# Ten effective feed-forward weights made during attention, and another order of copies and sums around the first layer norm's slices

## The reference

```python
Q = (layernorm(x) @ Wq.T).reshape(b, s, 8, 4, 128)
K = (ctx @ Wk.T).reshape(b, s, 8, 128)
V = (ctx @ Wv.T).reshape(b, s, 8, 128)
probs = softmax(where(causal, einsum('bqhed,bkhd->bheqk', Q, K) * scale, min))
x = x + tanh(g_xattn) * (einsum('bheqk,bkhd->bqhed', probs, V).reshape(b, s, 4096) @ Wd.T)

def linear(x, w, su, sv):              # su: (rows, 4), sv: (4, columns)
    return einsum('bsh,oh->bso', x, w * (su @ sv))
h = layernorm(x)
d = silu(linear(h, gate...)) * linear(h, up...)       # 1792 hidden units
x = x + tanh(g_ffn) * linear(d, down...)
```

## Time and profile before

| | us |
|---|---|
| median of 3 runs | 1369.67 (1368.61 to 1370.26) |
| the profiled execution | 1369.36 |
| its span, first to last instruction | 1367.6 |
| PE busy | 1359.0 (99%) |
| DVE busy | 960.1 (70%) |
| POOL busy | 955.9 (70%) |
| ACT busy | 561.9 (41%) |
| granted TensorE clock, mean | 1.000 |

### The profile page before, as it was taken

How to read it: one execution, slowest core, us unless ns; L and a number is a source line. 1 busy time by engine, 2 the same in 40 slices (tenths; PEclk the granted TensorE clock), 3 DMA queues, 4 the chain that set the end, 5 groups by cost and what they waited for, 6 DMA issues and landing times.

```text
span 1367.6 us, 21475 instructions
## 1 busy us (share of the span) xinstructions
PE 1359.0 (99%) x7794; PEld 1114.2 (81%) x7794; DVE 960.1 (70%) x1467; ACT 561.9 (41%) x952; POOL 955.9 (70%) x883
## 2 busy tenths in 40 slices
PE   9999999999999999999999999999999999999998
PEld 9988788888888878777787877788888888888887
DVE  6587776675555676676667877774789888766776
ACT  6455555545344432232323433332344434334333
POOL 5699999999887946445554666573787787666664
PEclk9999999999999999999999999999999999999999
DMA  8486777777978866453454556621322331311121
GB/s 294 138 266 203 252 251 252 262 244 242 341 252 284 293 228 222 153 167 124 153 171 140 185 158 197 200 71 39 78 62 62 93 85 47 123 54 47 48 69 70
DMA packets 158201, 226.47 MB, mean 166 GB/s; under 512 B 43280, under 2 KB 89872, under 8 KB 156048
## 3 DMA queue, kind: packets, MB, share of 16 engines
q1 hardware_dynamic: 157952, 224.83, 51.3%
q10 hardware_dynamic: 144, 0.26, 0.1%
HBM read 155.32 MB, written 69.73 MB: 165 GB/s over the span
## 4 chain that ended last, share of the span: by engine, by line
PE 83%; POOL 11%; DVE 2%; issue 2%; ACT 1%; DMA 1%; SPq 0%; DVEq 0%; ACTq 0%; POOLq 0%
PE bank L620 65%; POOL wa_lo L1702 5%; PE bank L898 4%; PE bank L900 4%; PE bank L899 4%; PE bank L776 4%; PE bank L752 3%; POOL ws L1690 1%; POOL ws L1693 1%; POOL ws L1691 1%; POOL ws L1695 1%; DVE xc L1291 1%; PE bank L667 0%; POOL xb L1671 0%; DMA er_raw<-in_sf_r 0%
## 5 line engine op out<-in xcount | busy, mean ns | idle before, releaser
L620 PE MATMUL bank<-xc,wa_hi 128*128 128x512 f32 x896 | 277.8, 391 | 0.8 <-ACT s L1023 0.8
L620 PE MATMUL bank<-wd_hi,o_hi 128*128 128x512 f32 x512 | 202.9, 396 | 0.5 <-issue 0.5
L620 PE MATMUL bank<-wd_lo,o_hi 128*128 128x512 f32 x512 | 199.6, 390 | 0.0
L620 PE MATMUL bank<-wd_hi,o_lo 128*128 128x512 f32 x512 | 199.2, 389 | 0.0
L620 PEld LDWEIGHTS bank<-xc,wa_hi 128*128 128x128 f32 x896 | 167.3, 188 | 38.0 <-ACT s L1023 2.6
L620 PE MATMUL bank<-xc,wa_lo 128*128 128x512 f32 x448 | 174.6, 390 | 0.0
L1074 ACT ACTIVATE o_hi<-bank 128x512 fp32r<-128x512 f32 x128 | 69.5, 595 | 228.3 <-PE bank L776 151.1
L1494 DVE SCALAR_TENSOR_TENSOR X<-bank,tg,X 128x512 f32<-128x512 f32 x221 | 154.4, 741 | 0.0
L620 PE MATMUL bank<-x_hi,wf_hi 128*128 128x512 f32 x392 | 152.7, 389 | 0.1
L620 PE MATMUL bank<-x_hi,wf_lo 128*128 128x512 f32 x392 | 152.5, 389 | 0.0
L620 PE MATMUL bank<-x_lo,wf_hi 128*128 128x512 f32 x364 | 141.7, 389 | 0.0
(11 more groups left out here) (182 smaller groups left out, 3160.8 us busy)
## 6 DMA issues: line engine op xcount, KB each, us to landing
q_scratch<-q_st SPq DMA_DIRECT2D x32, 1024.0 KB, 5.0
q_sb<-q_scratch SPq DMA_DIRECT2D x64, 512.0 KB, 4.7
w_raw<-in_wq SPq DMA_DIRECT2D x32, 512.0 KB, 4.3
wd_raw<-in_wd SPq DMA_DIRECT2D x16, 1024.0 KB, 4.9
f_raw<-ffn_eff_scratch SPq DMA_DIRECT2D x28, 512.0 KB, 3.6
er_raw<-in_sf_r SPq DMA_DIRECT2D x42, 256.0 KB, 4.3
e_raw<-in_wf SPq DMA_DIRECT2D x42, 256.0 KB, 5.6
ffn_eff_scratch<-e_eff SPq DMA_DIRECT2D x42, 256.0 KB, 5.5
```

What stands on the lines that cost most here:

```text
L620: last = pe.matmul(to, a, b, start=(start and n == 0), stop=(stop and n == 3 * len(pairs) - 1), skip_group_check=onto)
```

## The change

It has two parts.

**Effective weights.** `E_AT` now covers quads 12 to 43 alone (weights 0 to 31), so that quads 0 to 6 and 9 to 11 have none. The remaining ten (`E_LATE`, weights 32 to 41) are made in attention periods 4 to 13. There the product goes to bank 2 instead of 7, between `output(2u-7)` and `output(2u-6)`, behind a wait for DVE's addition of an earlier block; DVE's lo pair stands behind `out_lo(u-3)`, its multiplication behind `add_to_x(2u-7)`; ACT copies the factors behind `out_hi(u-3)`; the next period's weighted values, which write bank 2, wait for the multiplication. SP loads the factors and the raw tile for a period at the end of the one before and stores the product in the next period. These ten have buffers of their own. In the quads SP now issues the factors behind `store_q` and ahead of `store_e` and `load_e`. POOL's sums of weight group 1 no longer wait for a lo pair, and the waits of the attention's first period count the effective weights made by then.

**First layer norm.** In the quads of `COLUMNS` from 8 on (9, 13, 17, 21, 25) ACT copies product 1 to `s1` ahead of `left_hi` and not behind it. In quad 9 the columns are copied behind the quad's first result block. For slices 3 to 7 `x_hi` stands at the end of its quad and not in its middle, and `x_sums` moves from the end of the `COLUMNS` quad into the next quad, between `left_lo` and `left_sums`.

```diff
-    E_GAP = (NV - 1, NV)
-    E_AT = {q: m for m, q in enumerate(q for q in range(NQ) if q not in E_GAP)}
+    E_AT = {q: q - Q0 for q in range(Q0, NQ)}
+    NE = len(E_AT)
+    E_LATE = {4 + n: NE + n for n in range(NP - NE)}
+    X_LATE = 3
...
     def quad_dmas(q):
...
-            if m:
-                store_e(m - 1)
-                load_e(m)
+            if q + 1 in E_AT:
+                load_lr(E_AT[q + 1])
+            if q in E_AT:
+                if E_AT[q]:
+                    store_e(E_AT[q] - 1)
+                load_e(E_AT[q])
             if q + 6 < len(LOADS):
                 load_c(q + 6)
-            if q in E_AT and m + 1 < NP:
-                load_lr(m + 1)
...
             load_v(u - 1)
+            if p - 1 in E_LATE:
+                store_e(E_LATE[p - 1])
...
+            if p + 1 in E_LATE:
+                if p + 1 == min(E_LATE):
+                    for n in range(2):
+                        sp.wait_ge(d_qo[n], 16 * NB * NHP // 2)
+                load_lr(E_LATE[p + 1])
+                load_e(E_LATE[p + 1])
...
             if u == 0:
                 pe.wait_ge(v_turn, 4)
-                pe.wait_ge(v_e, NP)
+                pe.wait_ge(v_e, NE)
             elif u == 2:
                 pe.wait_ge(v_turn, 6)
+            elif u % 2 == 0 and u // 2 + 1 in E_LATE:
+                pe.wait_ge(v_e, E_LATE[u // 2 + 1] + 1)
...
             output(2 * u - 7)
+            if p in E_LATE:
+                pe.wait_ge(v_o, 2 * u - 4)
+                effective(E_LATE[p])
             output(2 * u - 6)
...
         def quad(q):
             w = q - NV
-            if -1 <= w < NW - 1 and q < NQ - 1:
+            copy_first = q in COLUMNS and w >= 0
+            copied_first = copy_first and q - 1 in X_SPLIT
+            if -1 <= w < NW - 1 and q < NQ - 1 and not copy_first:
                 left_hi(w + 1)
...
             a.activation(s1[:, :], bank[0][:, :], ACT.Copy).then_inc(a_s1, 1)
-            if q == 0:
-                lr_hi(0)
+            if copy_first:
+                left_hi(w + 1)
...
-            if q in X_SPLIT:
+            if q in X_SPLIT and X_SPLIT[q] < X_LATE:
                 x_hi(X_SPLIT[q])
-            if q in COLUMNS:
+            if q in COLUMNS and not copied_first:
                 x_columns(COLUMNS[q])
...
             a.activation(result(q, 0, 0), split(q, bank[0][:, :]), ACT.Copy).then_inc(a_c11, 1)
+            if copied_first:
+                x_columns(COLUMNS[q])
...
                 lr_hi(E_AT[q + 1])
+            if q in X_SPLIT and X_SPLIT[q] >= X_LATE:
+                x_hi(X_SPLIT[q])
...
             out_hi(u - 3)
+            if p in E_LATE:
+                lr_hi(E_LATE[p])
...
             out_lo(u - 3)
+            if p in E_LATE:
+                lr_lo(E_LATE[p])
             add_to_x(2 * u - 8)
...
             add_to_x(2 * u - 7)
+            if p in E_LATE:
+                effective(E_LATE[p])
...
             if w >= 2:
                 g.wait_ge(a_wa, 3 * (w - 1))
-            if w == 1:
-
-                g.wait_ge(v_lr, 2 * E_MOVE)
...
                 left_lo(w + 1)
+            if q in X_SPLIT and X_SPLIT[q] >= X_LATE:
+                x_sums(X_SPLIT[q])
...
-            if q in COLUMNS:
+            if q in COLUMNS and COLUMNS[q] < X_LATE:
                 x_sums(COLUMNS[q])
```

More of the change, by code:

```diff
@@ L129, in flamingo @@
     t2 = at(199, "t2", [P, BT])
[L130 to L135, removed]
+    er_raw = [at(205, "er_raw0", [P, D]), at(183, "er_raw1", [P, D])]
+    el_raw = [at(207, "el_raw0", [P, P]), at(187.5, "el_raw1", [P, P])]
+    e_raw = [at(161, "e_raw0", [P, D]), at(185, "e_raw1", [P, D])]
+    e_eff = [at(19, "e_eff0", [P, D]), at(179, "e_eff1", [P, D])]
+    er = [at(21, "er0", [P, D], F32R), at(181, "er1", [P, D], F32R)]
+    el = [at(2, "el0", [P, P], F32R), at(187, "el1", [P, P], F32R)]
     q_sb = [at(3, "q_sb0", [P, 2, CB, 2, S]), at(7, "q_sb1", [P, 2, CB, 2, S])]
@@ L227, in flamingo, with e_bank @@
     LOADS = [0, 1, 2, 3, *range(1, NCH)]
-    E_GAP = (NV - 1, NV)
-    E_AT = {q: m for m, q in enumerate(q for q in range(NQ) if q not in E_GAP)}
-    E_MOVE = E_AT[NV + 1]
+    E_AT = {q: q - Q0 for q in range(Q0, NQ)}
+    NE = len(E_AT)
+    E_LATE = {4 + n: NE + n for n in range(NP - NE)}
+    def e_bank(m):
+        return bank[2] if m >= NE else bank[7]
     STATS = {q: m for m, q in enumerate((0, 3, 5, 7, 11, 15, 19, 23))}
     APPLY, COLUMNS, X_SPLIT = ({q + n: m for q, m in STATS.items()} for n in range(1, 4))
+    X_LATE = 3
     WD_FIRST = range(NQ - 8, NQ - 4)
@@ L407, in load_lr @@
                 sp.wait_ge(v_lr, 2 * m)
[L408 to L412, removed]
+            sp.dma_start(el_raw[m >= NE][:, :], sf_l[m]).then_inc(d_lr, 16)
+            sp.dma_start(er_raw[m >= NE][:, :], sf_r[m]).then_inc(d_lr, 16)
         def load_e(m):
@@ L416, in load_e @@
                 sp.wait_ge(v_e, m)
-            if m == E_MOVE:
+            else:
                 sp.wait_ge(p_p[3], NV)
-            sp.dma_start(e_raw[m >= E_MOVE][:, :], wf[m]).then_inc(d_e, 16)
+            sp.dma_start(e_raw[m >= NE][:, :], wf[m]).then_inc(d_e, 16)
         def store_e(m):
             sp.wait_ge(v_e, m + 1)
-            sp.dma_start(ed[m], e_eff[:, :]).then_inc(d_eo, 16)
+            sp.dma_start(ed[m], e_eff[m >= NE][:, :]).then_inc(d_eo, 16)
         def store_q(q):
@@ L482, in _ @@
         load_x(0)
-        load_lr(0)
-        load_e(0)
         load_c(4)
@@ L522, in _ @@
                 store_q(q)
-                store_e(NP - 1)
+                store_e(NE - 1)
                 load_v(2)
@@ L666, in effective @@
                 pe.wait_ge(v_e, m)
-            pe.matmul(bank[7][:, :], el[:96, :], er[:96, :], start=True, stop=True).then_inc(p_e, 1)
+            pe.matmul(e_bank(m)[:, :], el[m >= NE][:96, :], er[m >= NE][:96, :], start=True, stop=True).then_inc(p_e, 1)
         pe.wait_ge(v_ident, 1)
@@ L1012, in lr_hi @@
                 a.wait_ge(p_e, m)
-            a.activation(el[:, :], el_raw[m >= E_MOVE][:, :], ACT.Copy).then_inc(a_lr, 1)
-            a.activation(er[:, :], er_raw[m >= E_MOVE][:, :], ACT.Copy).then_inc(a_lr, 1)
+            n = m >= NE
+            a.activation(el[n][:, :], el_raw[n][:, :], ACT.Copy).then_inc(a_lr, 1)
+            a.activation(er[n][:, :], er_raw[n][:, :], ACT.Copy).then_inc(a_lr, 1)
         def quad(q):
             w = q - NV
-            if -1 <= w < NW - 1 and q < NQ - 1:
+            copy_first = q in COLUMNS and w >= 0
+            copied_first = copy_first and q - 1 in X_SPLIT
+            if -1 <= w < NW - 1 and q < NQ - 1 and not copy_first:
                 left_hi(w + 1)
@@ L1059, in output_hi @@
                     a.wait_ge(p_p[3], NQ)
-                    a.wait_ge(v_e, NP)
+                    a.wait_ge(v_e, NE)
             a.activation(wd_hi[k % 2][:, e, :], wd_raw[:, e, :], ACT.Copy).then_inc(a_wd, 1)
@@ L1294, in lr_lo @@
             v.wait_ge(a_lr, 2 * (m + 1))
-            n = m >= E_MOVE
-            for to, raw, part in ((el, el_raw[n], slice(64, 96)), (er, er_raw[n], slice(32, 64))):
+            n = m >= NE
+            for to, raw, part in ((el[n], el_raw[n], slice(64, 96)), (er[n], er_raw[n], slice(32, 64))):
                 v.tensor_tensor(to[part, :], raw[part, :], f32(to[part, :]), ALU.subtract).then_inc(v_lr, 1)
@@ L1303, in effective @@
                 v.wait_ge(d_eo, 16 * m)
-            v.tensor_tensor(e_eff[:, :], bank[7][:, :], e_raw[m >= E_MOVE][:, :], ALU.mult).then_inc(v_e, 1)
+            n = m >= NE
+            v.tensor_tensor(e_eff[n][:, :], e_bank(m)[:, :], e_raw[n][:, :], ALU.mult).then_inc(v_e, 1)
         def quad(q):
@@ L1312, in quad @@
             v.tensor_tensor(t1[:, :], bank[1][:, :], s1[:, :], ALU.add).then_inc(v_t1, 1)
-            if q == 0:
-                lr_lo(0)
             if q in APPLY:
@@ L1394, in out_lo @@
             if u == 3:
-                v.wait_ge(d_eo, 16 * NP)
+                v.wait_ge(d_eo, 16 * NE)
             for n in range(2):
```

1 line of the change is left out of this document (removed).

## The result

| | before | after |
|---|---|---|
| median of 22 runs, us | 1368.78 | 1371.12 |
| ratio, 95% interval | | 1.0017 (1.0012 to 1.0023) |
| span of the profiled execution, us | 1367.6 | 1369.6 |

The change makes the kernel slower by 0.17%, some 2.3 us. That lies within the range and, by the bound of 0.2%, in the class given the highest chance; the forecast said +0.3. The sum came out near in part by luck: three of its terms were wrong, one by -1.8 us, one by +2.4 and one by +1.1, and only 1.7 of these 5.3 us was left in it. The wait that was to carry most of the loss, PE's for POOL's `left_lo`, came to some 0.4 us only.

A forecast was written before the change was run, and what follows sets the result against it. PE's work and stalls bound the kernel, with POOL 0.33 us behind at quad 28. -1.9 there and +2.3 in attention gave +0.4, taken as 1370.0 us; range 1366.0 to 1373.4.

The forecast's parts named there:

- The stalls removed: PE's stalls in quads 4 (0.83), 9 (1.09) and 17, 21, 25 (1.62) go: 3.54 us, the most the change can win.
- the bound of 330.6: Start of quad 28 if PE alone set it: 336.46 less 3.54 of stalls and 2.3 of products.
- What `s1` passes: The copy delays `left_hi` by 0.47, so POOL's idle place grows from 2.15 to 2.62 in quads 17, 21, 25: +1.4 us.
- What POOL gains: Seven of the ten removed lo pairs each free POOL by 0.45 us before quad 13: -3.15, bounds -1.35 and -4.5.
- 25.37 us of unbroken work: POOL's stretch from `left_lo` of quad 25, put at 309.1, to the end of `left_lo` for quad 28, taken as unchanged.
- the 334.6 forecast: Start of quad 28 as paced by POOL's `left_lo`, against 336.46 before: -1.9 us.
- rival A: POOL does not bind: quad 28 starts near 330.6, all 3.54 us go, time 1366.1 to 1367.2, taken as 1366.5; chance 0.17.
- The move of `x_sums` at nothing: Moving `x_sums` past one `left_lo` changes the order in POOL's stretch before quad 28, not its sum: 0 us.
- SP, taken as 0: In the quads `e_raw` lands 2 to 3 us later behind the factor loads; at worst one stall of 0.54, taken as 0.
- Attention, 2.3: The ten products moved into attention cost PE +2.3 us; no stall taken, bounds 0 and 0.54 for each of ten periods.
- rival D: DVE's multiplication comes late in attention and PE waits at each of ten weighted values: +4, so 1374; chance 0.12.
- Rival C: SP's effective weight loop becomes longer than a quad, 0.4 over in each of 31 quads: +12.4, about 1382; chance 0.05.

The follow-up runs named there:

- the combined version: Weights' part alone plus quad 9's key copy early, SP's old order, and attention's factor copies and lo pair ahead of the output's second half: 1366.05 us, ratio 0.9983.
- the first experiment: Changed kernel with its first layer norm part undone, so the weights' part alone: 1367.98 us, ratio 0.9995 to the kernel before.
- the seventh experiment: Kernel before with the lo pairs of effective weights 1 to 9 cut to 32 columns, all else as it was: 1365.86 us, ratio 0.9979.
- the sixth experiment: Weights' part alone plus product 1's copy ahead of the roundings in quads 13 to 25 and quad 9's key copy early: 1370.62 us, ratio 1.0017.
- the fourth: Changed kernel with the column sums back at the end of their quad, the rounding staying late: 1371.67 us, ratio 1.0019 to the kernel before.
- the third experiment: Changed kernel with SP's old order in all quads, store and load of the effective weight ahead of the factor loads: 1369.59 us, ratio 1.0011.
- the eighth experiment: Kernel before with one edit, quad 9's column copy put behind the key copy: 1369.1 us, ratio 1.0003.

## Why the prediction came out as it did

- **The stalls removed** (-3.54): right in number, wrong in cause for 1.62 of it. Quad 4's and quad 9's stalls went, and `s1` came earlier. It is also short of the most that can be won, as it leaves out small gaps: the combined version, which lost only 0.35 us in quads 12 to 28, has quad 28 at 330.17, ahead of the bound of 330.6. The three stalls of quads 17, 21 and 25 vanish in the first and the seventh experiment with the copy left where it was. They were POOL's pace, seen on ACT; what I said of quad 28 ("PE comes earlier and meets POOL") held for those too, and I did not draw it.
- **What `s1` passes**: right. POOL's idle place was to be 2.62 and is 2.64, and the sixth experiment shows the step to cost 2.6 us even with quad 9's gain beside it.
- **What POOL gains** (-3.15): too small. POOL came to quad 13 4.2 us earlier (189.09 to 184.90). Nine lo pairs, cut and not removed wholly, are worth 2.7 of that; the other 1.5 I have not separated from what the missing products and the other order on SP do.
- **25.37 us of unbroken work**: this was the false step behind the size of the term, together with the gain above. I carried POOL's rounds over from the trace as if their length were fixed. They are 40.56 before, 39.85 in the first experiment, 41.02 in the fourth, all with the same operations, and 40.99, 40.16 and 41.02 in the changed kernel. `left_lo` of quad 25 started at 307.07 and not at 309.1, and from there to the end of `left_lo` for quad 28 it took 23.33 us, to 330.40. So that operation was done 2.03 us ahead of PE, and the path that I gave for quad 28 was not the one that bound. The one that did went through the weight sums, ACT's rounding, the copy to `s1` and `x_lo`, as shown with the result. That quad 28 came out no further from 334.6 is luck in part. Quad 28 started at 332.43, between the 334.6 forecast and the 330.6 of rival A. With the stall of 0.4 in quad 28 itself 2.2 us were given back by this count, against 4.0 forecast. This put the kernel 1.8 us better than said. The Trainium skill, "SBUF — State Buffer", section "Who interferes with whom", says that the one who issues first has the shared port for its whole instruction; I weighed it only for the size of a lo pair, where I should have asked what order of issue each phase gives. The trace agrees in the shift's case: in the last section POOL's 0.20 us become 0.72 and end 0.05 behind DVE's instruction.
- **The move of `x_sums` at nothing**: right in the sum within the noise, as the fourth experiment shows (1371.67 with the sums back, 1371.12 without). The wait was another for it: the stalls of PE in quads 19, 20, 27 and 28 come by way of the sums' new place, and without the move PE waits for `left_lo`, most of all in quads 19, 23 and 27, which is the path that the forecast gave.
- **SP, taken as 0**: wrong by 2.4 us in the profiled execution and by 1.5 in the medians of the third experiment, the latter with intervals of about 1.2 us to either side. I bounded it by one short stall of 0.54. I had seen that `e_raw` comes later, not that the waiting factor load delays the whole queue, nor that in the last two quads the multiplication stands ahead of the additions.
- **Attention, 2.3**: under-sized by 1.1. 0.9 of that is the lo pair, 0.18 in every second period, at the product itself; the margin behind the multiplication, on which rival D rested, was sufficient. My bound of 0 to 0.54 a period covered it.
- **Rival C** did not come in general. `e_raw` lands faster now, some us behind the 1 MB store and no longer right behind it, as the medians of the profile's page show (KB each, us to landing; before, then after). On PE it showed in two quads of one experiment.

```profile
e_raw<-in_wf SPq DMA_DIRECT2D x42, 256.0 KB, 5.6
```

```profile
e_raw<-in_wf SPq DMA_DIRECT2D x42, 256.0 KB, 3.6
```

So: -1.8 in quads 12 to 28, +2.4 in quad 43, +1.1 in attention against the forecast's +0.4 make 2.1, which the trace has (2.0).

## What to carry to other kernels

When an engine that is not the bottleneck has no idle time, it paces the others at one remove: a stall on PE with ACT's name on it can be POOL's, and moving ACT's work then helps nobody, while half a microsecond put ahead of what POOL waits for costs double. Look for the rounds (the time from one fixed place to its like four quads on) of each nearly full engine and compare them with PE's. A DMA issue that waits at the head of a queue is a delay for every transfer behind it; look at what lands last at the far end of the queue, not at the load that was moved. And the check of a stall's cause is one edit that removes the load on the suspected engine (here nine lo pairs) and leaves the visible waiter alone.

## What the runs showed of the hardware

The same operations of POOL take 39.85 or 40.57 us for four quads, by where DVE's instructions with two SBUF inputs fall against POOL's. In the eighth experiment both forms stand in one execution: `left_lo` at 189.20, 229.77, 269.61 and 310.19, rounds of 40.57, 39.84 and 40.58. Its first two rounds have the same 34 operations, which start within 0.02 us of each other but for the last three. From the first round, the wide remainder on which `x_lo` falls, and the shift's multiplication just ahead of the idle place, with DVE's lo pair; then the same from the second:

```profile
210.36 4.23 POOL L1704 TENSOR_TENSOR wa_lo<-ws,wa_hi 128x1024 fp32r<-128x1024 f32 x1
226.89 0.72 POOL L1665 TENSOR_TENSOR shift<-neg_mean,rstd 128x2 f32<-128x2 f32 x1
...
226.88 0.68 DVE L1299 TENSOR_TENSOR er<-er_raw,er 32x512 fp32r<-32x512 f32 x1
```

```profile
250.93 4.24 POOL L1704 TENSOR_TENSOR wa_lo<-ws,wa_hi 128x1024 fp32r<-128x1024 f32 x1
267.25 0.20 POOL L1665 TENSOR_TENSOR shift<-neg_mean,rstd 128x2 f32<-128x2 f32 x1
...
267.74 0.28 DVE L1299 TENSOR_TENSOR el<-el_raw,el 32x128 fp32r<-32x128 f32 x1
```

The shift takes 0.72 where it is issued 0.01 us behind the larger half of a lo pair, and 0.20 where it runs ahead of the pair. That is 0.52 us. The last two weight sums give the other 0.2: they take 1.27 and 0.74 in the first round and 0.73 and 1.08 in the second.

What `x_lo` costs POOL does not set the form. It is about 1.8 us either way, in both rounds above on the wide remainder (4.23 for a quiet 2.40), and in the rounds of the weights' part alone, which are short too, on a sum (2.54 for 0.74):

```profile
244.91 2.84 POOL L1723 TENSOR_TENSOR wa_lo<-ws,wa_hi 128x1024 fp32r<-128x1024 f32 x1
247.70 2.54 POOL L1711 TENSOR_TENSOR ws<-w_raw 128x256 f32<-128x256 f32 x1
```

In the short form POOL's round equals PE's to 0.01 us, though POOL waits for PE nowhere in it. It is not a fixed length of POOL's: in the combined version the rounds are 39.63, 39.70 and 39.84, while PE's stay at 39.85. I take it that the contention with DVE, which PE paces, holds POOL in step, but that is argued and not shown.
